# One SP queue reordered, one transfer given another home, and the last batches of layer 3 regrouped, in a four-layer conditional network

## The reference

```
x = x + (x @ W_base.T + b_base + lora(x, cond) * 2)                  # layer 0
x = x + (x @ (sum_g cond[b,g] * weight[g] * mask).T + bias)          # layer 1
x = x + sum_k w[b,k] * (gelu(x @ gate_k) * (x @ up_k)) @ down_k + shared_mlp(x)   # layer 2, top 2 of 8
x = x + (silu(x @ Wu[e].T + bu) * (x @ Wg[e].T + bg)) @ Wd[e].T + bd # layer 3, e = argmax
```

## Time and profile before

| what | us |
|---|---|
| median of 3 runs | 82.08 (81.43 to 83.1) |
| the profiled execution's own time | 81.98 |
| its span, first to last instruction | 80.3 |
| PE busy | 75.9 (95% of the span) |
| DVE, ACT, POOL busy | 53.9, 49.2, 50.3 |
| the chain that ended last | PE 80%, DMA 8%, SPq 5%, DVE 2% |

### The profile page before, as it was taken

How to read it: one execution, slowest core, us unless ns; L and a number is a source line. 1 busy time by engine, 2 the same in 40 slices (tenths; PEclk the granted TensorE clock), 3 DMA queues, 4 the chain that set the end, 5 groups by cost and what they waited for, 6 DMA issues and landing times.

```text
span 80.3 us, 1590 instructions
## 1 busy us (share of the span) xinstructions
PE 75.9 (95%) x480; PEld 68.0 (85%) x480; DVE 53.9 (67%) x118; ACT 49.2 (61%) x99; POOL 50.3 (63%) x48
## 2 busy tenths in 40 slices
PE   6999999999999999999994999999999999997990
PEld 6979998888888998988882989989989989996990
DVE  1489679969565638177796939499399498436371
ACT  6420796879855896737999069456496550539160
POOL 3021366298999999999999999985639910000000
DMA  1998288999999995599988998989999679882102
GB/s 17 320 380 343 45 309 328 392 426 429 425 392 411 383 395 203 126 377 347 382 226 231 361 354 295 245 316 301 382 340 270 201 179 232 289 198 63 52 21 65
DMA packets 9367, 22.17 MB, mean 276 GB/s; under 512 B 1040, under 2 KB 5776, under 8 KB 9360
## 3 DMA queue, kind: packets, MB, share of 16 engines
q1 hardware_dynamic: 9072, 21.30, 77.9%
q10 hardware_dynamic: 288, 0.79, 2.5%
HBM read 17.88 MB, written 0.52 MB: 229 GB/s over the span
## 4 chain that ended last, share of the span: by engine, by line
PE 80%; DMA 8%; SPq 5%; DVE 2%; issue 1%; ACT 1%
PE bank L964 16%; DMA x_t<-p 8%; PE bank L950 5%; PE bank L947 5%; PE bank L948 5%; PE bank L979 5%; SPq L259 5%; PE bank L900 5%; PE bank L908 5%; PE bank L916 5%; PE bank L937 4%; PE bank L994 4%; PE bank L831 4%; PE bank L839 3%; PE bank L869 2%; PE bank L923 2%
## 5 line engine op out<-in xcount | busy, mean ns | idle before, releaser
L362 POOL TENSOR_TENSOR pair_low<-pair_w,wide_h 128x512 fp32r<-128x512 f32 x18 | 22.7, 1291 | 3.2 <-ACT wide_h L457 3.2
L419 ACT ACTIVATE gelu<-bank 128x512 f32<-128x512 f32 x24 | 14.1, 594 | 10.2 <-PE bank L950 7.1
L694 DVE SCALAR_TENSOR_TENSOR hid<-gelu,wsel,bank 128x512 f32<-128x512 f32 x16 | 11.8, 735 | 6.2 <-PE bank L950 2.0
L947 PE MATMUL bank<-wide_h,x_h 128*128 128x512 f32 x28 | 11.5, 409 | 0.0
L367 POOL TENSOR_TENSOR hid_l<-hid,hid_h 128x512 fp32r<-128x512 f32 x8 | 10.2, 1289 | 1.8 <-ACT hid_h L470 1.8
L948 PE MATMUL bank<-wide_h,x_l 128*128 128x512 f32 x28 | 10.9, 390 | 0.0
L708 DVE STREAM_TRANSPOSE p<-hid 128x512 f32<-128x512 f32 x14 | 10.0, 712 | 1.1 <-DMA x_t<-p 0.7
L457 ACT ACTIVATE wide_h<-pair_w 128x512 fp32r<-128x512 f32 x18 | 10.4, 622 | 0.4 <-DMA pair_w<-in_skill 0.2
L429 ACT ACTIVATE half<-bank,half_bias 128x128 f32<-128x128 f32 x12 | 3.7, 364 | 8.7 <-PE bank L979 4.4
L692 DVE TENSOR_TENSOR hid<-gelu,bank 128x512 f32<-128x512 f32 x8 | 5.5, 685 | 3.6 <-POOL hid_l L367 2.7
L964 PE MATMUL bank<-x_t,pair_w 128*128 128x128 f32 x40 | 5.5, 280 | 1.6 <-DMA x_t<-p 1.6
(11 more groups left out here) (120 smaller groups left out, 160.1 us busy)
## 6 DMA issues: line engine op xcount, KB each, us to landing
pair_w<-in_skill SPq DMA_DIRECT2D x11, 768.0 KB, 6.9
w<-in_layer SPq DMA_DIRECT2D x6, 384.0 KB, 8.9
x_t<-p SPq DMA_DIRECT2D x16, 128.0 KB, 3.3
b_mix<-p SPq DMA_DIRECT2D x12, 128.0 KB, 4.3
shared_sb<-in_skill SPq DMA_DIRECT2D x1, 768.0 KB, 11.8
home_x<-in_skill SPq DMA_DIRECT2D x1, 768.0 KB, 12.6
home_h<-in_skill SPq DMA_DIRECT2D x1, 768.0 KB, 4.4
home_l<-in_skill SPq DMA_DIRECT2D x1, 768.0 KB, 6.6
```

The costliest lines, as they stand in the source:

```text
L362: pool.tensor_tensor(low_of(b, k)[:, m, :], w[:, m, :], wide_h[:, ring_at(b, k) % RING, m, :].bitcast(fp32), ALU.subtract).then_inc(wide_l ...
L419: act.activation(gelu[:, n, :], ps[:, :], ACT.Gelu_apprx_tanh).then_inc(gelu_ready, 1)
L694: dve.scalar_tensor_tensor(hid[:, n, :], gelu[:, n, :], wsel[:, bass.DynSlice(weight, 1)], u_ps[n][:, :], ALU.mult, ALU.mult).then_inc(hid ...
L947: pe.matmul(ps[:, :], x2_h[:, S * b:S * (b + 1)], wide_h[:, n % RING, m, :], start=True, stop=False)
```

## The change

On SP, swap(1) goes ahead of load(5,0) and load(5,1). On PE, down3(0,0) goes ahead of down(1,0). The swap of batch 7 writes to `hid_last`, the first two thirds of home 4, whose last user is expert (2,0); so it waits for down(2,0) and no longer for down(5,1). Layer 3 of batch 6 has its first up product in `bank[4]` and no longer in `bank[7]`, and that one waits for nothing of batch 5; the second up product and the gates wait as before. Its four products stand together ahead of down(7,0); down3(5,1) goes behind down(7,1). The only wait on `silu3_ready` left on PE is ahead of the last gate product of batch 7, which shares `bank[4]`. On DVE, result(5,1) goes behind the product of batch 6.

```diff
+        hid_last = pair_w[:, 4, 0:2, :].rearrange("c m (a k s) -> c (m a) k s", k=TOP_K, s=S)
...
         def up3_ps(b, c):
+            if b == B - 2:
+                return (bank[4], bank[7])[c]
             return (bank[3], bank[2])[c] if is_last(b) else bank[7]
...
+        def hid_t_of(b):
+            return hid_last if is_last(b) else hid_t[b % 2]
...
-                    if b - 2 in TURNED:
+                    if is_last(b):
+                        sp.wait_ge(down_done, down_at(2, 0))
+                    elif b - 2 in TURNED:
                         sp.wait_ge(down_done, down_at(b - 2, 1))
                     for a in range(T):
-                        sp.dma_start(hid_t[q][:, a, :, :], turned[q][QUAD * a:QUAD * (a + 1), :, :, :]).then_inc(swapped[q], 16)
+                        sp.dma_start(hid_t_of(b)[:, a, :, :], turned[q][QUAD * a:QUAD * (a + 1), :, :, :]).then_inc(swapped[q], 16)
...
                 load(4, 1)
+                swap(1)
                 load(5, 0)
                 load(5, 1)
-                swap(1)
                 sp.wait_ge(down_done, down_at(0, 0))
                 load(6, 0)
                 swap(2)
...
                 result(B - 4, 0)
-                result(B - 3, 1)
                 residual(B - 1)
                 gated_silu3(B - 2, 0)
+                result(B - 3, 1)
                 gated_silu3(B - 1, 1)
...
-                        by_chunk = hid_t[b % 2][:, :, k, :].rearrange("p a (t s) -> p t a s", s=QUAD)
+                        by_chunk = hid_t_of(b)[:, :, k, :].rearrange("p a (t s) -> p t a s", s=QUAD)
...
-                    if c == 0 and at_least(b, 1) and not is_last(b):
+                    if c == (1 if b == B - 2 and n == 0 else 0) and b >= 1 and not is_last(b):
                         pe.wait_ge((hid3_ready if b <= IN_BANK else half3_ready, gate3_ready)[n], HC * b)
+                    if is_last(b) and n == 1 and c == 1:
+                        pe.wait_ge(silu3_ready, 1)
...
+                down3(0, 0)
                 down(1, 0)
-                down3(0, 0)
                 down(1, 1)
...
                 down3(B - 4, 0)
-                product3(B - 2, 0, 0, 0)
+                layer3(B - 2)
                 down(B - 1, 0)
+                down(B - 1, 1)
                 down3(B - 3, 1)
-                down(B - 1, 1)
-                pe.wait_ge(silu3_ready, 1)
-                product3(B - 2, 0, 0, 1)
-                both_chunks3(B - 2, 0, 1)
                 both_chunks3(B - 1, 1, 0)
                 both_chunks3(B - 1, 1, 1)
```

## The result

| | us |
|---|---|
| kernel before, median (beside this one) | 82.59 (81.43 to 83.52, 4 runs) |
| changed kernel, median | 88.88 (88.0 to 90.36, 4 runs) |
| ratio | 1.079, 95% interval 1.057 to 1.100 |
| profiled execution after: time, span | 89.35, 86.5 |

The ratio compares only the executions of the faster of two states, 88.00 and 88.42 us against 81.43 and 82.08, and the profiled execution of 89.35 us is not among them.

A forecast was written before the change was run, and what follows sets the result against it. PE was taken to bound the kernel, with the DMA queue second at its limit. 81.98 + 2.6 (late swap(2)) - 0.35 (tail) = 84.2 us; own range 83.2 to 85.3, wider range 82.2 to 85.6.

The forecast's parts named there:

- The bound and the gain: PE bounds; swap(1) lands earlier, down3(0,0) runs first, and PE is ready for down(2,0) 1.15 us earlier.
- The queue behind swap(1): Swap(2) finds three loads ahead, not one; down(2,0) starts 2.6 us later (2.0 to 3.2), PE idle 3.8 us.
- The 0.2 us by which runs were said to scatter: Whole runs: scatter of 0.2 us between them, counted into the forecast's own range.
- PE's clock falls in the stall: Rival, ahead of down(2,0): PE's clock drops while it stands idle; no idle time before exceeded 1.6 us; chance 0.06.
- The tail: Batches 6 and 7 at the end: reordered products and the earlier swap(7) gain 0.35 us (0 to 0.65).
- Moving result(5,1) behind batch 6's product costs nothing that is waited for: DVE in the tail: no cost, since down3(6,0) needs it at 76.8, when it is done.
- What was named as cover: ACT, POOL, DVE's turn(4,0) and SP's later swaps: delays hidden or in step with PE's, counted at zero.

The follow-up runs named there:

- experiment 3: Changed kernel with 16 more matmuls of zeros on PE between gate_up_wide(4,1) and down(2,0); 85.68 us, ratio 1.045.
- Experiment 4: Changed kernel with SP's list load(5,0), swap(1), load(5,1), so two loads stand ahead of swap(2); 83.28 us, ratio 1.018.
- experiment 2: Kernel before with one edit, swap(1) ahead of the two loads of batch 5 on SP; 87.55 us, ratio 1.066.
- experiment 6: Changed kernel with SP's list as before, plus a PE wait for swap(3) ahead of down(2,0); 87.36 us, kernel before 82.10.
- Experiment 8: Changed kernel with SP's list as before, plus an output tile of its own for batch 7; 81.65 us, ratio 0.996.
- Experiment 5: Changed kernel with swap(2) put ahead of load(5,1) in SP's list; 84.69 us, ratio 1.033.

## Why the prediction was wrong

**The bound and the gain: right.** Swap(1) landed 3.0 us after its last piece (forecast 2.9). down(1,0) followed down3(0,0) with no wait, and PE was ready for down(2,0) 15.5 us after the issue into `home_h` (48.21 - 32.72), before after 16.7 (48.61 - 31.89): 1.2 us, where 1.15 was forecast. That the two agree so closely is partly luck: experiment 3, the same kernel up to there, was ready after 16.0, 0.7 us less than before.

**The queue behind swap(1): right in kind, too small.** From the issue of load(5,0) I had swap(2) landing 10.5 us later; it took 10.9. The start of down(2,0) was forecast 2.6 us late and was 3.0, the stall 3.8 and was 4.2. Experiment 4 confirms the step with another number of loads, and experiment 2 that nothing else is needed. The loads landed 1.9 to 2.4 us apart, around the 2.10 of the earlier trace rows. A higher price stood in the rows too: of the three loads of before the last landed 6.0 us behind the first (42.3 - 36.3), 3.0 us for each. Experiment 3, in which only the wait is left, came to 1.045 (1.035 to 1.055), where the forecast was 1.026; in its profile down(2,0) starts 20.35 us after the issue into `home_h`, 3.6 later than before. So this term of the sum, 2.6 us, measured 3.0 to 3.6 in the profiles, and by the timed runs the forecast was some 1.5 us too low even with the clock held. The 0.2 us by which runs were said to scatter was too small as well: the three runs of before lie between 81.43 and 83.1.

**The step that failed: the clock.** The prediction had it as a rival, "PE's clock falls in the stall", with its place and a chance of 0.06. The sum of the forecast has nothing for it. It was the case that came. Measured it cost 2.6 us in the profiled execution and 1.5 in those of experiments 2 and 6. The two compared executions of the changed kernel have the mean clock of the latter, 0.98, and no profile, so how their 4 us of miss divide between clock and wait is open; both terms were short. The clock fell in all four runs of the changed kernel and all four of experiment 2; experiment 3 took it away by filling the same stall, and experiment 6 brought it back with no transfer moved. The reasoning for 0.06 was that the clock had held at 1.6 us. But I had just worked out an idle time of 3.8 us, more than twice the longest in the trace, and for that the trace had no say. The trace after has it: 4.23 us idle for a DMA, and 0.50 in the windows from 52 to 58. At that clock the work from 48.61 to 51.41, 2.8 us, would take 2.8 more. With this estimate the forecast would have been 84.2 + 2.8 = 87.0, 1.2 us under the 88.2 of the compared executions.

**The tail: half of it at most, and a step that failed.** Forecast -0.35, measured -0.05 to -0.18. down(7,0) came 4.36 us after down(6,0), by the forecast 4.4 (73.4 - 69.02), and the new home brought nothing, as worked out. The sentence "Moving result(5,1) behind batch 6's product costs nothing that is waited for" was wrong. I followed PE's wait for it and not SP's: result(5,1) starts 7.18 us after down(6,0) (82.61 - 75.43), before 5.92 (74.94 - 69.02), so its store left later, and batch 7's sum waits 0.46 us for that store to land because it shares the tile. Experiment 8 shows 0.21 us for it; with it the tail is 0.26 to 0.39 shorter than before, about the forecast.

**What was named as cover held.** ACT waited 2.9 us for load(5,0), and POOL's subtractions stayed ahead of PE: that of expert (5,1) ended at 52.3, and PE came to that expert at 59.1. The delays of PE and SP kept step, 6.4 us from 59 us to the tail, and no later swap made PE wait. DVE's turn(4,0) waited 3.46 us for swap(2), as was said. Experiment 5 shows how thin that cover is: with load(5,1) 2 us later still, it is the bound.

## What to carry to other kernels

When a transfer is moved ahead of others in a queue, count what now stands ahead of the *next* waiting transfer, at the measured time for each. Here the one that was moved forward landed 3.0 us after its last piece (before 3.8), and the next one paid, with 7.3 (before 4.2). If the sum gives a wait of PE longer than any in the trace, its clock is part of the forecast and not a remote rival: here it went to 0.50 and was back at 1.00 after 4.0 and 5.8 us of work behind the wait, in the profiles of experiment 2 and of the changed kernel, and that cost 1.5 and 2.6 us. That the clock held at a wait of 1.6 us did not settle it for one of 4.2. And when a result is put later, follow its store and the next writer of its tile, not only the engine that reads the result.

## What the runs showed of the hardware that was not expected

- PE's granted clock fell in 8 of 8 runs of the kernels whose profiles show PE idle for 4.2 and 4.1 us, and in 3 of 4 where the profile shows 3.4 us. With 2.5 us it held in 4 of 4, yet with 0.9 and 2.2 us close together it fell in 2 of 4. The idle times are those of the one profiled run of each kernel. In the changed kernel it was still at half when PE had been at work for 5 us, and what a fall cost differed: 2.6 us there, 1.5 in experiments 2 and 6.
- With matmuls of zeros in the stall it was 1.00 in 4 of 4 runs (experiment 3), where the changed kernel without them had 0.96 to 0.98.
- Behind a backlog on SP's queue, loads of 768 KB landed in the order of issue, 1.9 to 2.4 us apart in the changed kernel and 2.7 and 3.2 in the one before, and a swap's last piece landed 1.3 to 1.5 us behind the load ahead of it, in the same two traces. Its first pieces do not always stay behind: in the kernel before that of swap(1) landed at 40.9 (37.83 + 3.1) and that of swap(3) at 49.8 (46.31 + 3.5), 1.4 and 1.3 us ahead of the load issued before each. PE waits for all four pieces, each of which lands in 16 parts in the trace (down(1,0) started at 43.72, after the last at 43.6), so this did not help.
- The same eight PE instructions at the start lasted 2.16 to 3.68 us from one execution to another, before anything that the kernels differ in. That is more than the gains that were looked for in the tail.
